# Layer 0 of a two-layer cross-attention kernel: transfers in another order, on other queues

## The chip, the cores and the metric

The kernel runs on one NeuronCore of a Trainium2 chip. Its time is the device time of one execution in microseconds (us). TensorE (PE in the profile; PEld is its weight loading) does the matmuls and the transposes, VectorE (DVE), ScalarE (ACT) and GpSimd (POOL) work element by element, and SyncE (SP) only issues DMAs. ScalarE issues DMAs as well, between its own instructions. Each of the two has a queue of its own, `q1` for SyncE and `q10` for ScalarE; 16 DMA engines serve both. Engines wait for one another through semaphores.

## The reference

Two layers run one after the other on a batch of 8 sequences, `x` (8, 112, 512), with a context `ctx` (8, 375, 512). All is float32. Layer 0 is a grouped-query cross-attention with 32 query heads and 8 key/value heads of 16 elements:

```python
q = x @ Wq + bq ; k = ctx @ Wk + bk ; v = ctx @ Wv + bv
scores = einsum('bkgld,bksd->bkgls', q, k) * 0.25 + mask
out = einsum('bkgls,bksd->bkgld', softmax(scores), v)
x = layernorm(out @ Wo + bo + x) * gamma + beta
```

Layer 1 is two cross-attentions of 16 heads with 128 elements, each on a layer norm of `x`, and a GELU MLP with 2048 hidden units, with residuals. It is about nine tenths of the time, and the change doesn't touch its arithmetic.

## The kernel before

**Tiling.** The batch is done in two halves (`hf` 0 and 1) of four sequences, one after the other, and each half runs layer 0, both attentions of layer 1 and the MLP. For float32 accuracy each operand is split into a high and a low part (`_hi`, `_lo`), and a product is three matmuls (lines 794 to 796). Weights come into two slots of `raw`; GpSimd splits them (lines 674 and 676) and frees the slot, which the next load awaits.

**Layer 0 before its loop.** TensorE works through a list of units, written out by hand (`pre_order`): `n` transposes of the context ("natural" layout), `k` keys of a sequence, `q` a quarter of the queries (one 128-column piece of Wq each), `vt` and `v` values. ScalarE takes the high part of each result and VectorE the low part. For the first half the list is `n0 k0 n1 k1 n2 vt0 k2 q0 vt1 v0 n3 q1 vt2 v1 k3 q2 vt3 v2 q3 v3`, for the second `k0 q0 k1 q1 vt0 q2 vt1 v0 k2 q3 vt2 v1 k3 vt3 v2 v3`. Keys and queries are then rearranged through DRAM: `store_keys0` (line 440, four DMAs) and `store_queries0` (line 455, two DMAs) write scratch tensors, and `load_keys0` (line 449) and `load_queries0` (line 474, four DMAs) read them back in the layout of the scores. A store waits for its unit; a load waits for its store to land. SyncE issues all of these, the loads of the weights (line 418) and the mask (line 498) in the order in which they are written, so one that waits holds those behind it. The first load of queries also waits for a memset of `qo` on GpSimd (line 661), which comes after the splits of Wq. A store of the natural layout (`nat_scratch`, 1536 KB) goes out on ScalarE's queue (line 1251). ScalarE frees `keys` buffers by waiting for the earlier stores to land.

**The layer-0 loop.** It has 128 steps `n`, 32 for each of four chunks `c`, eight for each sequence `b` of a chunk. In a step TensorE forms the scores of one head and transposes the probabilities of an earlier one, VectorE takes the maximum (line 1730), ScalarE the exp (line 1331), and each second step ScalarE and VectorE move two transposed heads into a buffer `pt0` (lines 1177 and 1566). There are two such buffers of four heads, used in turn: number 0 is `pt_hi`/`pt_lo`, where pieces 1 to 3 of the queries stood before (`q0_split`), number 1 lies in `rr`, where two of the natural stages stood. So ScalarE waits at step 1 until all stores of queries have landed, and at step 4 until the natural stores have, in the first half also the write of the extra values (`bx_scratch`, line 574). Each eight steps GpSimd scales a batch of outputs (line 685). The keys and queries of a later chunk are loaded once TensorE has read the same sequence of the chunk before, 24 steps ahead of their use.

**The second half's inputs.** In the first half the context and the tokens of the second are copied inside DRAM (`ctx_copy`, 3000 KB, line 585; `x_copy`, 896 KB, line 487), on SyncE's queue behind the loads of the second chunk; they are read back at the end of layer 1. There ScalarE splits the tokens (`split_x`), and at the end of the half stores `out` (line 1556) and then the last natural stage.

## Time and profile before

| | us |
|---|---|
| median of 3 runs | 2464.18 |
| lowest and highest | 2464.01, 2466.08 |
| the profiled execution | 2464.88 |
| its span, first to last instruction | 2463.0 |
| TensorE busy | 2320.6 |
| VectorE busy | 1401.3 |
| ScalarE busy | 999.3 |
| GpSimd busy | 765.6 |

Mean granted TensorE clock: 0.981 of full speed. The first half starts at 0 and its layer-0 loop at 69; the second starts at about 1254 and its loop at about 1290. A timeline line gives the start, the busy time, the engine, the line, what is written from what, and in brackets the idle time before it with what ended it. A line of SPq or ACTq is a DMA issue: the time is that of issuing, not of the transfer. A line of windows gives the busy time of each engine in a stretch, then the granted clock, the mean busy share of the 16 DMA engines and their GB/s.

### The profile page before, as it was taken

The numbers are of one execution on the slowest core, as the hardware profiler recorded it, in microseconds if no ns is written. First come the engines' busy times: TensorE is split into PE (matmuls) and PEld (weight loads), VectorE is DVE, ScalarE is ACT, GpSimd is POOL, SyncE is SP. The second block draws the span as 40 slices with busy tenths as digits, with TensorE's granted clock in tenths as the row PEclk, the third lists the DMA queues.
The fourth block names the chain that finished last, engine by engine and source line by source line (L and its number), as shares of the span: only waits on it lengthen the run. The fifth ranks groups of instructions, "written<-read, shape, count | busy, mean of one in ns | idle before, by whom it ended". The sixth has DMA issues, their size and how long they took to land. (4 is left out here: it accounts for less than half of the span.)

```text
span 2463.0 us, 36589 instructions
## 1 busy us (share of the span) xinstructions
PE 2320.6 (94%) x13464; PEld 2087.0 (85%) x13464; DVE 1401.3 (57%) x3146; ACT 999.3 (41%) x2195; POOL 765.6 (31%) x823
## 2 busy tenths in 40 slices
PE   6898899999999999998988979999999999999998
PEld 5666899998989999997876769998989999998976
DVE  4687645454565455456548965455546655454574
ACT  3685433243433333243238944243334333243420
POOL 2132322415141423313531331414141422415055
PEclk9899999999999999999999989999999999999999
DMA  8351323233323323234363213333332323233222
GB/s 279 96 156 39 92 85 108 87 91 116 99 86 96 95 82 111 82 96 146 125 198 96 77 40 95 97 101 97 103 95 82 96 90 107 86 87 121 79 76 79
DMA packets 134533, 250.46 MB, mean 102 GB/s; under 512 B 31151, under 2 KB 54831, under 8 KB 133335
## 3 DMA queue, kind: packets, MB, share of 16 engines
q1 hardware_dynamic: 90863, 125.37, 17.0%
q10 hardware_dynamic: 43496, 122.76, 16.2%
q8 instruction: 110, 1.80, 0.3%
q14 instruction: 64, 0.52, 0.1%
HBM read 223.19 MB, written 29.48 MB: 103 GB/s over the span
## 5 line engine op out<-in xcount | busy, mean ns | idle before, releaser
L674 POOL TENSOR_SCALAR wk_hi<-raw 128x512 fp32r<-128x512 f32 (+1 forms) x84 | 54.0, 643 | 905.5 <-DMA raw<-in_wk 747.5
L1411 ACT ACTIVATE probs<-scores,prm 112x376 f32<-112x376 f32 x256 | 147.1, 575 | 342.9 <-DVE prm L1805 342.8
L794 PE MATMUL pj_two<-ctx_hi,wk_hi 128*128 128x376 f32 x708 | 243.6, 344 | 7.7 <-DVE rr L1566 4.1
L1566 DVE TENSOR_TENSOR rr<-pj_two,rr 128x448 fp32r<-128x448 f32 (+2 forms) x223 | 147.0, 661 | 172.6 <-ACT rr L1177 172.2
L795 PE MATMUL pj_two<-ctx_lo,wk_hi 128*128 128x376 f32 x708 | 239.0, 338 | 0.0
L796 PE MATMUL pj_two<-ctx_hi,wk_lo 128*128 128x376 f32 x708 | 238.5, 337 | 0.0
L794 PE MATMUL pj_two<-pt_hi,nat 125*128 125x448 f32 x531 | 198.8, 374 | 10.6 <-issue 10.2
L676 POOL TENSOR_TENSOR wb_lo<-raw,wb_hi 128x512 fp32r<-128x512 f32 x152 | 197.9, 1302 | 12.7
L1568 DVE SCALAR_TENSOR_TENSOR k_lo<-pj_two,cur,k_hi 128x375 fp32r<-128x375 f32 x167 | 101.3, 607 | 173.1 <-ACT k_hi L1179 172.6
L796 PE MATMUL pj_two<-pt_hi,nat 125*128 125x448 f32 x531 | 195.4, 368 | 0.0
L795 PE MATMUL pj_two<-pt_lo,nat 125*128 125x448 f32 x531 | 195.2, 368 | 0.0
L1179 ACT ACTIVATE k_hi<-pj_two,cur 128x375 fp32r<-128x375 f32 x167 | 95.6, 573 | 228.4 <-PE pj_two L796 223.6
L799 PE MATMUL tp_two<-ident,probs 112*126 112x112 f32 (+1 forms) x1152 | 163.0, 266 | 25.8 <-ACT probs L1331 12.2
L799 PEld LDWEIGHTS tp_two<-ident,probs 112*126 112x126 f32 (+1 forms) x1152 | 146.2, 160 | 47.7 <-DVE probs L1813 15.7
L1177 ACT ACTIVATE rr<-pj_two 128x448 fp32r<-128x448 f32 (+2 forms) x223 | 127.4, 572 | 129.6 <-PE pj_two L796 110.9
L1566 DVE TENSOR_TENSOR pt_lo<-tp_two,pt_hi 126x336 fp32r<-126x336 f32 (+1 forms) x288 | 144.2, 537 | 24.7 <-ACT pt_hi L1177 24.7
L674 POOL TENSOR_SCALAR wb_hi<-raw 128x512 fp32r<-128x512 f32 x152 | 98.8, 650 | 188.9 <-DMA raw<-in_wv 76.8
L1805 DVE TENSOR_REDUCE prm<-scores 112x1 f32<-112x376 f32 x256 | 138.5, 541 | 21.7 <-PE scores L796 21.7
L1331 ACT ACTIVATE probs<-probs,prm 112x375 f32<-112x375 f32 x256 | 146.9, 602 | 2.6 <-DVE prm L1730 2.6
L794 PEld LDWEIGHTS pj_two<-ctx_hi,wk_hi 128*128 128x128 f32 x708 | 134.5, 190 | 9.9 <-issue 4.5
L676 POOL TENSOR_TENSOR wo<-raw,wo 128x512 fp32r<-128x512 f32 x104 | 139.0, 1337 | 8.7
L1177 ACT ACTIVATE pt_hi<-tp_two 126x336 fp32r<-126x336 f32 (+1 forms) x288 | 123.5, 478 | 42.5 <-PE tp_two L799 29.1
(278 smaller groups left out, 6611.1 us busy)
## 6 DMA issues: line engine op xcount, KB each, us to landing
nat<-nat_scratch ACTq DMA_DIRECT2D x256, 384.0 KB, 3.7
raw<-in_wq SPq DMA_DIRECT2D x72, 256.0 KB, 3.3
raw<-in_wo SPq DMA_DIRECT2D x72, 256.0 KB, 2.6
raw<-in_wk SPq DMA_DIRECT2D x64, 256.0 KB, 3.8
raw<-in_wv SPq DMA_DIRECT2D x64, 256.0 KB, 4.2
raw<-in_w SPq DMA_DIRECT2D x64, 256.0 KB, 2.9
nat_scratch<-rr ACTq DMA_DIRECT2D x7, 1536.0 KB, 8.8
k_hi<-keys_scratch SPq DMA_DIRECT2D x32, 188.0 KB, 2.8
```

The source lines that it names most:

```text
L674: nc.gpsimd.tensor_scalar(hi, src, 1.0, 0.0, ALU.mult, ALU.add).then_inc(split_hi, 1)
L676: nc.gpsimd.tensor_tensor(lo, src, hi.bitcast(F32), ALU.subtract).then_inc(signal, k)
L794: nc.tensor.matmul(dst, l_hi, r_hi, start=first, stop=False)
L795: nc.tensor.matmul(dst, l_hi, r_lo, start=False, stop=False)
L796: return nc.tensor.matmul(dst, l_lo, r_hi, start=False, stop=last)
L799: return nc.tensor.transpose(dst, src, ident[0:parts, 0:parts])
L1177: i = nc.scalar.activation(dst, src, ACT.Copy)
L1331: nc.scalar.activation(probs[0:L, n % 4, 0:S], probs[0:L, n % 4, 0:S], ACT.Exp, bias=neg_max[0:L, n % HPC:n % HPC + 1], scale=-1.0).then_i ...
L1411: nc.scalar.activation(probs[0:L, h, 0:SK], scores[n % SCR][0:L, 0:SK], ACT.Exp, bias=neg_max[0:L, h:h + 1], accum_out=row_sum[0:L, h:h + ...
L1566: i = nc.vector.tensor_tensor(dst, src, hi.bitcast(F32), ALU.subtract)
L1568: i = nc.vector.scalar_tensor_tensor(dst, src, bias, hi.bitcast(F32), ALU.add, ALU.subtract)
L1805: nc.vector.tensor_reduce(neg_max[0:L, h:h + 1], scores[n % SCR][0:L, 0:SK], AX_X, ALU.max, negate=True).then_inc(max_ready, 1)
```

## The change

It has six parts. In the first half SyncE issues the loads of Wq's pieces 1 to 3 each between the earlier stores and loads of keys, and the mask and the bias rows later; the stores of the queries come before the last load of keys. In the second half the load of queries comes before the store of keys 1, and each store of queries one place earlier. The two copies inside DRAM leave SyncE and are issued by ScalarE at step 24 of the first half's loop. The buffers `pt0` are used in the other order in the second half, and ScalarE's waits at steps 1 and 4 are exchanged there. The last natural stage is stored before `out`. All arithmetic is the same.

```diff
                     store_keys0(0, *pre_split("k", 0))
+                    load_q0(base + RAW_Q, 1)
+                    store_keys0(1, *pre_split("k", 1))
+                    load_q0(base + RAW_Q + 1, 2)
+                    load_keys0(0, 0)
+                    load_q0(base + RAW_Q + 2, 3)
+                    load_keys0(0, 1)
                     sp.dma_start(rows8_dram[0], bias_v).then_inc(rows8_in, 16)
                     sp.dma_start(rows8_dram[1], bv).then_inc(rows8_in, 16)
-                    store_keys0(1, *pre_split("k", 1))
-                    load_q0(base + RAW_Q, 1)
-                    load_keys0(0, 0)
-                    load_keys0(0, 1)
+                    store_keys0(2, *pre_split("k", 2))
+                    store_queries0(0, *pre_split("q", 0))
 
                     sp.wait_ge(pj_free, pre_freed("n", 2, SC - 1) + PJ)
                     load_mask()
-                    load_q0(base + RAW_Q + 1, 2)
-                    store_keys0(2, *pre_split("k", 2))
-                    store_queries0(0, *pre_split("q", 0))
-                    load_q0(base + RAW_Q + 2, 3)
                     load_queries0(0, 0)
...
                     store_queries0(1, *pre_split("q", 1))
+                    store_queries0(2, *pre_split("q", 2))
                     store_keys0(3, *pre_split("k", 3))
-                    store_queries0(2, *pre_split("q", 2))
+                    store_queries0(3, *pre_split("q", 3))
                     load_keys0(0, 3)
-                    store_queries0(3, *pre_split("q", 3))
                 else:
...
                     load_keys0(0, 0)
+                    load_queries0(0, 0)
+                    store_queries0(1, *pre_split("q", 1))
                     store_keys0(1, *pre_split("k", 1))
-                    load_queries0(0, 0)
                     load_mask()
-                    store_queries0(1, *pre_split("q", 1))
+                    store_queries0(2, *pre_split("q", 2))
                     load_keys0(0, 1)
-                    store_queries0(2, *pre_split("q", 2))
+                    store_queries0(3, *pre_split("q", 3))
                     store_keys0(2, *pre_split("k", 2))
-                    store_queries0(3, *pre_split("q", 3))
                     load_keys0(0, 2)
...
-                        if hf == 0:
-                            sp.dma_start(ctx_dram, ctx_t[:, HB:B, :]).then_inc(ctx_copied, 16)
-                            copy_x(1)
...
-                    p_hi, p_lo = (t[0:KC, :, s * L:(s + 1) * L] for t in pt0[u % 2])
+                    p_hi, p_lo = (t[0:KC, :, s * L:(s + 1) * L] for t in pt0[(u + hf) % 2])
...
-                    if n == 1:
+                    if n == (1, 4)[hf]:
 
                         for t in q0_out:
                             act.wait_ge(t, (hf + 1) * 32)
-                    if n == 4:
+                    if n == (4, 1)[hf]:
...
+                    if n == 24 and hf == 0:
+
+                        act.dma_start(ctx_dram, ctx_t[:, HB:B, :]).then_inc(ctx_copied, 16)
+                        act.dma_start(x_dram[:, T:2 * T], x_t[:, T:2 * T]).then_inc(x_copied, 16)
...
                             split_x(1)
+                            store_nat(1, m, mpj + mu["n", SC - 1] + 1)
...
-                if hf == 0:
-                    store_nat(1, HB - 1, at["mlp"] + (MLPG - 1) * MLP_U[0] + mu["n", SC - 1] + 1)
```

SyncE's queue in the first half, from the stores of keys 0 on. `raw<-in_wq` is a piece of Wq, `keys_scratch` a store of keys, `queries_scratch` one of queries (`rr` is piece 0), `k_hi` and `qo` are loads of keys and queries, `xacc<-in_mask` is the mask. Before:

```order
L440 DMA keys_scratch<-wk_hi 8x16x376 x4
L525 DMA bias_rows_scratch<-in_bias_v 16x256
L526 DMA bias_rows_scratch<-in_bv 16x256
L440 DMA keys_scratch<-wk_lo 8x16x376 x4
L418 DMA raw<-in_wq 128x4x128
L449 DMA k_hi<-keys_scratch 128x376 x2
L498 DMA xacc<-in_mask 112x4x375
L418 DMA raw<-in_wq 128x4x128
L440 DMA keys_scratch<-wk_hi 8x16x376 x4
L455 DMA queries_scratch<-rr 8x16x448 x2
L418 DMA raw<-in_wq 128x4x128
L474 DMA qo<-queries_scratch 32x4x448 x4
```

And with the change:

```order
L440 DMA keys_scratch<-wk_hi 8x16x376 x4
L418 DMA raw<-in_wq 128x4x128
L440 DMA keys_scratch<-wk_lo 8x16x376 x4
L418 DMA raw<-in_wq 128x4x128
L449 DMA k_hi<-keys_scratch 128x376
L418 DMA raw<-in_wq 128x4x128
L449 DMA k_hi<-keys_scratch 128x376
L531 DMA bias_rows_scratch<-in_bias_v 16x256
L532 DMA bias_rows_scratch<-in_bv 16x256
L440 DMA keys_scratch<-wk_hi 8x16x376 x4
L455 DMA queries_scratch<-rr 8x16x448 x2
L498 DMA xacc<-in_mask 112x4x375
```

The three pieces of Wq have moved up among the first two stores and loads of keys, and the mask stands behind the first store of queries.

SyncE's queue in the second half, from the load of keys 0 to the load of keys 2. Here `pt_hi` and `pt_lo` are the two parts of the query pieces 1 to 3. Before:

```order
L449 DMA k_hi<-keys_scratch 128x376
L440 DMA keys_scratch<-wk_lo 8x16x376 x4
L474 DMA qo<-queries_scratch 32x4x448 x4
L498 DMA xacc<-in_mask 112x4x375
L455 DMA queries_scratch<-pt_hi 8x16x448
L455 DMA queries_scratch<-pt_lo 8x16x448
L449 DMA k_hi<-keys_scratch 128x376
L455 DMA queries_scratch<-pt_hi 8x16x448
L455 DMA queries_scratch<-pt_lo 8x16x448
L440 DMA keys_scratch<-wk_hi 8x16x376 x4
L455 DMA queries_scratch<-pt_hi 8x16x448
L455 DMA queries_scratch<-pt_lo 8x16x448
```

And with the change:

```order
L449 DMA k_hi<-keys_scratch 128x376
L474 DMA qo<-queries_scratch 32x4x448 x4
L455 DMA queries_scratch<-pt_hi 8x16x448
L455 DMA queries_scratch<-pt_lo 8x16x448
L440 DMA keys_scratch<-wk_lo 8x16x376 x4
L498 DMA xacc<-in_mask 112x4x375
L455 DMA queries_scratch<-pt_hi 8x16x448
L455 DMA queries_scratch<-pt_lo 8x16x448
L449 DMA k_hi<-keys_scratch 128x376
L455 DMA queries_scratch<-pt_hi 8x16x448
L455 DMA queries_scratch<-pt_lo 8x16x448
L440 DMA keys_scratch<-wk_hi 8x16x376 x4
```

The last store of queries now precedes the four DMAs of keys 2, and the load of queries those of keys 1.

ScalarE where the halves meet, from the splits of the context and the tokens to the first keys of the second half. Before:

```order
L1220 ACTIVATE ctx_hi<-ctx_lo 128x4x375
L1225 ACTIVATE h_hi<-pt_hi 128x896
L1225 ACTIVATE h_hi<-pt_lo 128x896
L1556 DMA out<-xacc 112x4x512
L1251 DMA nat_scratch<-rr 128x3072
L1179 ACTIVATE wk_hi<-pj_two,prm 128x376
```

And with the change:

```order
L1217 ACTIVATE ctx_hi<-ctx_lo 128x4x375
L1222 ACTIVATE h_hi<-pt_hi 128x896
L1222 ACTIVATE h_hi<-pt_lo 128x896
L1248 DMA nat_scratch<-rr 128x3072
L1558 DMA out<-xacc 112x4x512
L1176 ACTIVATE wk_hi<-pj_two,prm 128x376
```

The natural store and the store of `out` have changed places; `out` alone waits for the last sums of the MLP.

## Rows read from the trace of the kernel before

**Rows 1.** The page: busy time, share of the span and instructions of each engine.

```profile
PE 2320.6 (94%) x13464; PEld 2087.0 (85%) x13464; DVE 1401.3 (57%) x3146; ACT 999.3 (41%) x2195; POOL 765.6 (31%) x823
```

**Rows 2.** Waits of TensorE: us in total, times, longest us.

```profile
PE tp_two L799 <- ACT probs L1331: 12.2, 2, 7.4
...
PE pj_two L794 <- POOL wb_lo L676: 6.7, 2, 3.7
```

**Rows 3.** Timeline of TensorE, layer 0 of both halves: start, busy us, what.

```profile
62.74 0.71 PE L794 MATMUL pj<-h_hi,wb_hi 128*128 128x448 f32 x1 [5.15 <-POOL wb_lo L676]
...
69.47 0.59 PE L930 MATMUL scores<-k_hi,qo 128*112 128x376 f32 x2 [1.27 <-DVE k_lo L1566]
...
1268.75 0.44 PE L794 MATMUL pj_two<-h_hi,wb_hi 128*128 128x448 f32 x1 [3.66 <-POOL wb_lo L676]
```

**Rows 4.** Timeline of GpSimd, first half, splits of Wq.

```profile
41.70 0.87 POOL L674 TENSOR_SCALAR wb_hi<-raw 128x512 fp32r<-128x512 f32 x1 [20.06 <-DMA raw<-in_wq]
...
60.63 0.62 POOL L674 TENSOR_SCALAR wb_hi<-raw 128x512 fp32r<-128x512 f32 x1 [8.76 <-DMA raw<-in_wq]
```

**Rows 5.** Timeline of SyncE's DMA issues, first half.

```profile
36.01 5.31 SPq L449 DMA_DIRECT2D k_hi<-keys_scratch  x2
...
46.84 1.57 SPq L455 DMA_DIRECT2D queries_scratch<-rr  x2
48.45 0.58 SPq L418 DMA_DIRECT2D raw<-in_wq  x1
59.90 1.76 SPq L474 DMA_DIRECT2D qo<-queries_scratch  x4
...
69.77 0.88 SPq L455 DMA_DIRECT2D queries_scratch<-pt_lo  x1
74.70 0.36 SPq L449 DMA_DIRECT2D k_hi<-keys_scratch  x1
```

**Rows 6.** Timeline of ScalarE, both halves.

```profile
80.79 0.73 ACT L1177 ACTIVATE pt_hi<-tp_two 125x672 fp32r<-125x672 f32 x1 [7.96 <-DMA queries_scratch<-pt_lo]
...
1255.24 0.51 ACTq L1251 DMA_DIRECT2D nat_scratch<-rr  x1
...
1298.49 0.73 ACT L1177 ACTIVATE pt_hi<-tp_two 125x672 fp32r<-125x672 f32 x1 [5.37 <-DMA queries_scratch<-pt_lo]
```

**Rows 7.** Timeline of GpSimd, first half's loop: one batch of outputs each.

```profile
129.52 0.40 POOL L685 TENSOR_TENSOR xacc<-xacc,prm 112x128 f32<-112x128 f32 x1 [3.63 <-DVE xacc L1739]
137.81 0.40 POOL L685 TENSOR_TENSOR xacc<-xacc,prm 112x128 f32<-112x128 f32 x1 [3.75 <-DVE xacc L1739]
148.57 0.41 POOL L685 TENSOR_TENSOR xacc<-xacc,prm 112x128 f32<-112x128 f32 x1 [10.36 <-DVE xacc L1739]
158.20 0.41 POOL L685 TENSOR_TENSOR xacc<-xacc,prm 112x128 f32<-112x128 f32 x1 [9.22 <-DVE xacc L1739]
```

**Rows 8.** DMA issues from 110 to 150: KB each, median us to landing.

```profile
ctx_copy<-in_ctx_t SPq DMA_DIRECT2D x1, 3000.0 KB, 15.0
```

**Rows 9.** Windows: us, PE, PEld, DVE, ACT, POOL busy, clock, DMA share, GB/s.

```profile
1250.00:1255.00 5.00, 5.00 (x25) 4.04 (x24) 3.12 (x8) 0.00 (x0) 3.25 (x4) 1.00 0.20 55
...
1260.00:1265.00 5.00, 5.00 (x28) 4.58 (x26) 1.29 (x2) 1.21 (x2) 0.00 (x0) 1.00 0.99 308
...
1270.00:1275.00 5.00, 5.00 (x21) 4.65 (x20) 0.68 (x1) 0.64 (x1) 3.87 (x2) 0.70 0.58 186
```

**Rows 10.** Timeline of GpSimd, second half: third piece of Wq, memset of the queries.

```profile
1266.64 0.62 POOL L674 TENSOR_SCALAR wb_hi<-raw 128x512 fp32r<-128x512 f32 x1 [6.98 <-DMA raw<-in_wq]
...
1270.93 3.09 POOL L661 MEMSET qo<- 128x3584 f32 x1 [0.15 <-POOL wb_lo L676]
```

**Rows 11.** Timeline of SyncE's DMA issues behind the copies and in the second half.

```profile
128.35 7.75 SPq L474 DMA_DIRECT2D qo<-queries_scratch  x4
...
1274.10 2.64 SPq L474 DMA_DIRECT2D qo<-queries_scratch  x4
...
1288.72 0.89 SPq L455 DMA_DIRECT2D queries_scratch<-pt_lo  x1
```

More of the change, by code:

```diff
@@ L1360, in _ @@
                         two = n // 2
-                        move(pt0[n // 4 % 2][0][0:KC, n % 4 - 1:n % 4 + 1, :], twos[two % 2][0:KC, :, 0:SC * L],
+                        move(pt0[(n // 4 + hf) % 2][0][0:KC, n % 4 - 1:n % 4 + 1, :], twos[two % 2][0:KC, :, 0:SC * L],
                              two_ready, two0 + two + 1, mid=two_mid)
@@ L1758, in _ @@
                         two = n // 2
-                        hi, lo = (p[0:KC, n % 4 - 1:n % 4 + 1, :] for p in pt0[n // 4 % 2])
+                        hi, lo = (p[0:KC, n % 4 - 1:n % 4 + 1, :] for p in pt0[(n // 4 + hf) % 2])
                         lo_of(lo, twos[two % 2][0:KC, :, 0:SC * L], hi, two_mid, two0 + two + 1, two_free)
```

## The prediction

> **What bounds the kernel now.** The page comes first [rows 1]: TensorE is busy 94% of the span, so time is to be had only where it stands idle or runs slowly. The waits of TensorE, largest in total first, then say for whom [rows 2]: 12.2 us in two waits for ScalarE's exps (longest 7.4), 6.7 us in two waits for GpSimd's splits of Wq (longest 3.7), and a third such wait on another buffer, below. All sit in the layer-0 stages at the start of either half. The timelines of the engines there give the causes.
>
> First half. TensorE waits 3.0 us at 41.1 (6.7 less the longest, 3.7) and 5.15 us at 57.6 for split columns of Wq [rows 2, 3]; GpSimd had waited 20.06 and 8.76 us for the raw columns to land [rows 4], because SyncE issues these loads behind stores of keys, the last one at 48.45 [rows 5]. The attention loop starts at 69.47 [rows 3] and stops at once: ScalarE waits 7.96 us at step 1 for the last queries store, which SyncE issues behind the load of keys 3 (74.70, [rows 5]), and goes on at 80.79 [rows 6]. In the loop GpSimd scales one batch each 8.3 us (129.52 to 137.81); the next two come 10.76 and 9.63 us apart [rows 7]. There the copies for the second half, 15.0 us to landing [rows 8], stand in SyncE's queue ahead of the keys and queries of the third chunk. The excess is 2.5 + 1.3 = 3.8 us.
>
> Second half. The last natural store leaves at 1255.24, right behind `out` [rows 6]; the share of the DMA engines is 0.20 before it and 0.99 after [rows 9]. GpSimd waits 6.98 us for the third piece of Wq [rows 10], TensorE 3.66 us for the split [rows 3], and its granted clock is 0.70 in the next 5 us against 1.00 in the 5 us that end as the wait begins [rows 9]. Then ScalarE waits 5.37 us at step 1 of the loop for the last queries store [rows 6], issued at 1288.72 [rows 11].
>
> **Part by part.** Positive is time saved.
>
> 1. First half, loads of Wq in front. Columns 1 are issued right behind the stores of keys 0. SyncE's queue is served about in order, and these stores had landed when the load that waits for them could go, at 36.01 [rows 5]. So columns 1 land near 37 instead of 41.7, are split some 2.2 us later [rows 4], and the wait of 3.0 goes. Columns 3 leave at about 36.4 instead of 48.45, and the wait of 5.15 goes. TensorE would reach the loop near 60. It can't use all of it: the loop needs the first queries from DRAM. Their store, issued at 46.84, had landed when SyncE issued the load, at 59.90 [rows 5], and the new order does not issue it earlier, since the landing of keys 1 stands ahead of it as before. But the mask (0.67 MB) no longer lies in front of it, and natural store 3 on ScalarE's queue comes 3 us earlier. I take 3.4 us: the load at 56.5.
>
> 2. First half, stores of queries in front of the load of keys 3. SyncE's issues end at 70.65 and go on at 74.70, when keys 3 has landed [rows 5]; the last queries store follows that. Now it goes ahead of it, and of the 4 us I take 2.6, since its bytes still queue. Items 1 and 2: 3.4 + 2.6 = **6.0 us**. Lower bound: 2.6 alone. Upper bound: both TensorE waits, 3.0 + 5.15, and a little clock, 9. Next in line are the extra values, which ScalarE awaits at step 4; their write follows the load of keys 3, now near 71 to 74 with landing near 77, and ScalarE gets there at about 78. There is no margin, so I stay at 6.0.
>
> 3. Copies on ScalarE's queue, at step 24 of the first loop, some 25 us after its start. SyncE's queue is rid of 3.9 MB, and the 3.8 us of [rows 7] go. The loads that now run beside the copies are those of the second chunk's last sequences. SyncE issues each as soon as its buffer is free, 24 steps ahead of its use, 25 us at 8.3 us for eight steps, and even the whole copy takes only 15.0 us to land [rows 8]. So they hide. The new cost is the issuing: the natural store took ScalarE 0.51 us to issue [rows 6], two such are 1.0; I take 0.9, all of it lost, as ScalarE is one of the engines that set the loop's pace. Net **2.9 us**, between 0 (loads still late) and 3.8 (issues hidden). Here the Trainium skill speaks against the change: DMA: Bandwidth & Descriptors, section Issuing engines are not separate DMA queues, says that transfers started by scalar and sync run on the same 16 engines and interleave, and that a second issuer saves only the time of issuing. By that rule the copies take the same bandwidth from the loads wherever they are issued. No copy on ScalarE's queue in the trace of before could show it; it is weighed as a rival.
>
> 4. Natural store in front of `out`. ScalarE issues it right after the token splits, near 1246, ahead of the stretch with a share of 0.20 [rows 9]. Nothing waits for its condition: its pieces were finished before. It takes 1.5 MB out of the stretch from 1255 to 1265, where Wq's pieces 2 and 3 are loaded. Against it, pieces 0 and 1 of Wq and Wv now load beside it, 2 to 3 us later, and about 1.3 us of wait could appear at piece 1. Of the 3.66 us and some 1.5 us of low clock (0.30 of 5 us) I take 3.5. The memset of the query rows, 1270.93 plus 3.09 [rows 10], ends when SyncE's load of queries leaves, 1274.10 [rows 11]; both move up by 3.3 us.
>
> 5. Second half, order of the stores and swapped buffers. At step 1 ScalarE now fills the buffer in `rr`, which needs only the natural stores, long landed; the queries' stores it needs at step 4, 3.3 us later. Before, from the load of queries to the landing of the last queries store: 3.9 MB from 1274.10 to 1298.4, 24.3 us, 160 GB/s. In the new order keys 1's stores come into that stretch and keys 2's leave it; the bytes are the same. From 1270.8 that gives 1295.1. The mask, with 2.8 MB up to its end at the same rate, lands at 1288.2 and lets the loop start then, 1.9 us sooner than VectorE's 1290.1; step 4 is reached at 1295. Before, it was reached at 1298.5 + 3.3 = 1301.8. Items 4 and 5: 1301.8 - 1295.1 = **6.7 us**. Lower bound: nothing gained before the loop, the last store landed at 1298.4 as before, 3.4. Upper bound: 5.37 + 3.66, 9. Next in line are keys 2 at step 16, landed at about 1299.5 and needed at 1302.
>
> Sum: 6.0 + 2.9 + 6.7 = **15.6 us**. The profiled execution took 2464.88 us, its span and 1.9 around it; that is 0.7 above the median of 2464.18. 2464.9 - 15.6 = **2449.3 us**. The stages behind are untouched and follow one another on TensorE, so what is gained at the start of a half arrives at the end.
>
> **Rivals.**
>
> Bytes decide, 2456.0. The stretches are bound by the flow through SyncE's queue, and another order of the same bytes moves the last landing little. For it: a share of 0.99 [rows 9] and 24.3 us for 3.9 MB. Against it: the hole in SyncE's queue from 70.65 to 74.70. Price: the lower bounds of both stages, 2.6 + 2.9 + 3.4 = 8.9.
>
> The copies still hurt, 2453.1. They slow the loads of the second chunk as they did those of the third, and the 3.8 us are not gained: 2464.9 - 15.6 + 3.8. Against it stand the 25 us of lead. This is what the skill's rule on issuing engines would give.
>
> New waits take the place, 2460. ScalarE waits at step 4 of the first loop for the extra values, TensorE at step 16 of the second for keys 2, each 5 to 6 us: left are 1 + 2.9 + 1. Against it: each producer also moves up.
>
> Slower, 2471.3. ScalarE's queue does not take the second copy until much of the first is through, and every us in which it holds ScalarE is lost to the loop. For it: on SyncE, four small loads behind the copies took 7.75 us to issue [rows 11]. Price: held for 20 us (15.0 to landing, and more beside other loads), and 2 us of low clock after it, with 0.9 for the issues, against 6.0 + 3.8 + 6.7: 2464.9 + 22.9 - 16.5. It decides from about 13 us of holding. Against it: SyncE issued the second copy without such a stop.
>
> **How the numbers follow.** Forecast 60%; bytes decide 20%; copies still hurt 8%; new waits 8%; slower 4%. The range leaves out the last two: its upper end, 2459, is 2464.9 less all lower bounds, 2.6 + 0 + 3.4; its lower end, 2443, less all upper bounds, 9 + 3.8 + 9. A measurement of this kernel can tell about 0.2%, 4.9 us, from no change, so faster means under 2459.3. The first three cases are faster, 88%; new waits is the same, 8%; slower 4%.
>
> **What the changed profile would show.** Item 1: no TensorE wait for a split of Wq in the first half, loop start at 61 to 66. Item 2: ScalarE's step 1 at 73 to 77. Item 3: batches 8.3 us apart throughout, one by under 1.5 us longer after the copies. Item 4: TensorE's wait for the third piece under 1.5 us, the share from 1250 to 1255 (less what the first half saves) near 0.9. Item 5: ScalarE at step 4 within 7 us of the loop's start. The prediction is wrong if the first queries store lands no earlier, if ScalarE takes over 2 us to issue the copies, or if its wait at step 4 of either half is over 3 us.

## The result

| | before | changed |
|---|---|---|
| median, 19 runs each | 2464.18 us | 2455.36 us |
| lowest, highest | 2457.64, 2472.16 | 2448.16, 2465.56 |
| profiled span | 2463.0 | 2453.3 |
| mean granted TensorE clock | 0.981 | 0.985 |

The ratio is 0.9964, with a 95% interval of 0.9955 to 0.9973: 8.9 us faster, between 6.7 and 11.1. The forecast was 15.6 us. Sign and range (2443 to 2459) were right, the size was not.

To see where the time went, five points of the two traces are compared. The first and the last batch that GpSimd scales mark a loop (as in [rows 7]), and the unit of keys 0 on ScalarE marks the start of the second half.

| us | before | changed | difference |
|---|---|---|---|
| first batch of loop 1 | 96.41 | 96.59 | +0.2 |
| loop 1, first to last batch | 124.24 | 120.42 | -3.8 |
| from there to keys 0 of the second half | 1035.48 | 1037.61 | +2.1 |
| from keys 0 to the first batch of loop 2 | 57.24 | 46.84 | -10.4 |
| loop 2 | 120.40 | 120.40 | 0 |
| from there to the end | 1029.23 | 1031.44 | +2.2 |
| span | 2463.0 | 2453.3 | -9.7 |

The third and the sixth row, mostly layer 1, are 84% of the span, somewhat less than the nine tenths given at the start.

Engine totals hardly move against [rows 1]; the work is the same. From the page of the changed kernel:

```profile
PE 2311.3 (94%) x13464; PEld 2078.5 (85%) x13464; DVE 1401.8 (57%) x3146; ACT 998.9 (41%) x2195; POOL 766.4 (31%) x823
```

**First half: nothing gained.** SyncE's issues in the changed kernel; they answer to [rows 5]:

```profile
22.84 11.67 SPq L440 DMA_DIRECT2D keys_scratch<-wk_lo  x4
34.55 0.77 SPq L418 DMA_DIRECT2D raw<-in_wq  x1
...
44.78 0.34 SPq L449 DMA_DIRECT2D k_hi<-keys_scratch  x1
...
49.98 2.98 SPq L455 DMA_DIRECT2D queries_scratch<-rr  x2
...
61.99 1.74 SPq L474 DMA_DIRECT2D qo<-queries_scratch  x4
...
74.02 0.87 SPq L455 DMA_DIRECT2D queries_scratch<-pt_lo  x1
78.68 0.36 SPq L449 DMA_DIRECT2D k_hi<-keys_scratch  x1
```

Piece 1 of Wq now stands in front of the stores of keys 1, and these four took 11.67 us to issue, against 9.31 before (10.6 to 14.0 in the six profiles with this order, 8.1 to 10.7 in the three with the old one). The load that waits for them goes at 44.78, and the queries of chunk 0 are stored at 49.98 instead of 46.84 and loaded at 61.99 instead of 59.90. TensorE, and then ScalarE at steps 1 and after, show what that means:

```profile
68.83 0.94 PE L927 MATMUL scores<-k_hi,qo 128*112 128x376 f32 x2 [9.07 <-DMA qo<-queries_scratch]
```

```profile
80.98 0.73 ACT L1174 ACTIVATE pt_hi<-tp_two 125x672 fp32r<-125x672 f32 x1 [8.36 <-DMA queries_scratch<-pt_lo]
```

Both waits of TensorE for splits of Wq are gone, as forecast. In their place stands one of 9.07 us for the queries themselves, and step 1 is as late as in [rows 6].

**Loop 1.** GpSimd's batches, at the place of [rows 7], and ScalarE's issues of the copies:

```profile
129.75 0.41 POOL L682 TENSOR_TENSOR xacc<-xacc,prm 112x128 f32<-112x128 f32 x1 [2.11 <-DVE xacc L1739]
138.03 0.40 POOL L682 TENSOR_TENSOR xacc<-xacc,prm 112x128 f32<-112x128 f32 x1 [3.72 <-DVE xacc L1739]
146.32 0.41 POOL L682 TENSOR_TENSOR xacc<-xacc,prm 112x128 f32<-112x128 f32 x1 [7.88 <-DVE xacc L1739]
```

```profile
105.23 0.59 ACTq L1364 DMA_DIRECT2D ctx_copy<-in_ctx_t  x1
105.86 0.63 ACTq L1365 DMA_DIRECT2D x_copy<-in_x_t  x1
```

Up to the last two, which are closer together in both kernels, all batches are 8.3 us apart. The whole 3.8 us are gained in this pair of profiles, and the 1.2 us of issuing cost nothing that can be seen. That is not so in every execution: in four later profiles the second copy took ScalarE 1.29 to 1.79 us to issue instead of 0.63, and one batch came 0.7 to 1.2 us late. One of them is of the changed kernel with another order only in its second half:

```profile
104.18 1.47 ACTq L1365 DMA_DIRECT2D x_copy<-in_x_t  x1
```

**Second half.** ScalarE stores natural early, at 1238.47, while SyncE is still issuing the loads of Wk (1233.59 to 1240.78). Then Wk lands later, GpSimd waits 5.45 us for it (1.41 before), and VectorE's low parts of Wk stand ahead of its last MLP sums, for which TensorE waits. GpSimd, then TensorE:

```profile
1246.04 0.41 POOL L698 TENSOR_SCALAR wk_hi<-raw 128x256 fp32r<-128x256 f32 x1 [5.45 <-DMA raw<-in_wk]
```

```profile
1247.87 0.48 PE L791 MATMUL pj_two<-wo,qo 128*112 128x512 f32 x1 [2.33 <-DVE xacc L1616]
```

The wait for the third piece of Wq [rows 3] is gone, as forecast, but the idle stretch of the DMA engines is only moved, and the low clock stands behind the new wait (0.66, against 0.70 in [rows 9]):

```profile
1248.00:1253.00 5.00, 5.00 (x17) 3.81 (x18) 3.03 (x4) 0.00 (x0) 3.72 (x3) 0.66 0.20 56
```

Behind that, on ScalarE: a new wait at the unit of keys 3, and step 1 without the 5.37 us of [rows 6]:

```profile
1280.13 0.57 ACT L1176 ACTIVATE wk_lo<-pj_two,prm 128x376 fp32r<-128x376 f32 x1 [3.86 <-DMA keys_scratch<-wk_lo]
...
1287.54 0.73 ACT L1174 ACTIVATE rr<-tp_two 125x672 fp32r<-125x672 f32 x1 [0.38 <-PE tp_two L796]
```

### The profile page after: what moved, and what is told of

The parts are those of the page before. It is cut to its first block and busy times, and to the rows that moved or that the text cites. A ratio compares the mean times of both kernels' runs of the same rounds, so it can differ in the third digit from the quotient of the medians.

```text
span 2453.3 us, 36589 instructions
## 1 busy us (share of the span) xinstructions
PE 2311.3 (94%) x13464; PEld 2078.5 (85%) x13464; DVE 1401.8 (57%) x3146; ACT 998.9 (41%) x2195; POOL 766.4 (31%) x823
## 5 line engine op out<-in xcount | busy, mean ns | idle before, releaser
L1730 DVE CUSTOM_DVE_ANT_0 probs<-scores,xacc 112x375 f32<-112x375 f32 x256 | 133.4, 540 | 12.9 <-PE scores L927 12.9
```

The lines of the kernel that those rows point to most:

```text
L1730: nc.vector.tensor_tensor_reduce(probs[0:L, n % 4, 0:S], scores[n % SCR][0:L, 0:S], mask_v[:, n // HPC % HB, :], -1.0, 3.0e38, ALU.add, AL ...
```

## The experiments

Two theories stood at the start: the order in SyncE's queue decides (then another order of the first half must pay), or the bytes do, whatever their order. Single profiles of kernels with the same start differ by up to 2.6 us at the first batch, and those with the same order at the change of halves by up to 5.5 us in the stretch of some 1035 us ahead of it, so totals and stretches of single profiles are read with that in mind, and means of several or the waits themselves are preferred. Of the experiments, those with stores by channel were run four times each and the one with the natural store put back ten times, the others once.

### One store earlier still

The first queries are stored ahead of keys 2, of the load of keys 1 and of the bias rows.

```diff
+                    store_queries0(0, *pre_split("q", 0))
+                    store_keys0(2, *pre_split("k", 2))
                     load_keys0(0, 1)
                     sp.dma_start(rows8_dram[0], bias_v).then_inc(rows8_in, 16)
                     sp.dma_start(rows8_dram[1], bv).then_inc(rows8_in, 16)
-                    store_keys0(2, *pre_split("k", 2))
-                    store_queries0(0, *pre_split("q", 0))
```

> The changed kernel, but in the first half the store of queries 0 comes ahead of the store of keys 2, and both come ahead of the load of keys 1 (which waits for the landing of keys 1, 44.78 in the changed kernel). Theory: that landing held the store of queries 0 (49.98) and so the first load of queries (61.99) and the loop. Then the store goes out at 39 to 41, the load of queries at 50 to 56, the loop starts at 60 to 63 (TensorE is ready at about 60), ScalarE passes step 1 at 73 to 76 instead of 80.98, and the first batch of outputs is scaled at 89 to 92 instead of 96.59. Rival, bytes decide: the queue is bound by its flow; the load goes at 58 or later and the first batch is within 2 us of 96.6.

Measured: one run of 2450.13 us; the first batch at 94.06. The store goes at 39.33 instead of 49.98 and the load at 52.35 instead of 61.99, 9.6 us earlier, yet TensorE still waits for it, until 65.76:

```profile
65.76 0.94 PE L927 MATMUL scores<-k_hi,qo 128*112 128x376 f32 x2 [8.37 <-DMA qo<-queries_scratch]
```

SyncE's last queries store is issued at 68.53 and ScalarE goes on at 78.46. Issued at 52.35, the four loads took 7.2 to 11.2 us to land. Of 9.6 us in the order 2.0 to 2.5 arrive at the first batch (94.06, against a mean of 96.03 over four profiles with the changed order, or 96.59), hardly more than the spread. The first theory is right on the issues and wrong on all that follows them: mostly the second. Something other than the order limits the flow.

### The copies at another time

```diff
-                    if n == 24 and hf == 0:
+                    if n == 44 and hf == 0:
```

> The changed kernel, but ScalarE issues the two copies at step 44 of the first loop, about 126 us, the time at which SyncE issued them before. It asks whether the queue or the time took the 3.8 us out of the loop. The loop from its first to its last batch took 124.2 us before and 120.4 in the changed kernel. If the queue decides (the loads of the third chunk no longer stand behind the copies but share the engines with them), 120.4 to 121.5. If only the time decides (same engines, same bytes beside the loads with the short lead), 123 to 125.

Measured: one run of 2460.97 us; loop 1 takes 120.53 us, against 120.42 with the copies at step 24. They are issued at 124.67 and 125.30, where SyncE issued them at 126.33 and 126.96 in the kernel before, beside the loop's loads, and hurt nothing in the loop. So it was SyncE's queue, in which four small loads stood behind them (7.75 us to issue, [rows 11]), and not the traffic. Beside the copies, but on another queue, the slowest four of these loads took 4.78 us to issue. The Trainium skill (DMA: Bandwidth & Descriptors, section Issuing engines are not separate DMA queues) says that a second issuer saves only the time of issuing, which is usually small beside the transfer. Read as in the rival, that nothing is gained in the loop, it is not borne out here: the loop is 3.7 us shorter in this profile. SyncE's time of issuing did fall, from 7.75 to 4.78 us, so a part of what was saved is of the kind that the rule names, but it was not small.

### The natural store alone, the second half's order alone

Two kernels, each the kernel before with one part of the change. First part 4, the store behind the last token split (its old place is taken out):

```diff
                             split_x(1)
+                            store_nat(1, m, mpj + mu["n", SC - 1] + 1)
```

> The kernel before with one part of the change: the last natural store in front of out. Theory: it delays the loads of Wk, Wq and Wv for the second half, GpSimd's split, VectorE's second part of Wk and with it the last sums of the MLP behind it on VectorE. From the last batch of the first loop to ScalarE's first keys of the second half it takes 1035.5 us before and 1037.6 in the changed kernel; here 1038 to 1041, and TensorE waits 2 to 3 us for VectorE's sums near 1250. From those keys to the loop's first batch it takes 57.2 before and 46.8 changed; here the wait for the third piece of Wq goes, 51 to 54, with the wait at step 1 still there. Rival: the store costs nothing there and the 4 us are run-to-run variation of layer 1: 1033 to 1036.

Measured: one run of 2465.82 us beside 2468.11 of the kernel before. From loop 1's last batch to keys 0 it took 1039.71 us (before 1035.48), from there to loop 2 54.61 (before 57.24). As expected, TensorE no longer waits for the third piece of Wq. The cost seen in the changed kernel is there, and step 1's wait stays:

```profile
1251.44 0.49 PE L794 MATMUL pj_two<-wo,qo 128*112 128x512 f32 x1 [2.35 <-DVE xacc L1615]
```

```profile
1297.57 0.73 ACT L1177 ACTIVATE pt_hi<-tp_two 125x672 fp32r<-125x672 f32 x1 [7.83 <-DMA queries_scratch<-pt_lo]
```

Then part 5, the order of the second half's stores with the exchanged pairs:

```diff
                     load_keys0(0, 0)
+                    load_queries0(0, 0)
+                    store_queries0(1, *pre_split("q", 1))
                     store_keys0(1, *pre_split("k", 1))
-                    load_queries0(0, 0)
...
-                    if n == 1:
+                    if n == (1, 4)[hf]:
```

> The kernel before with one part of the change: the order of the stores and loads in the second half and the swapped buffers with their waits. From ScalarE's first keys of the second half to the loop's first batch it takes 57.2 us before and 46.8 changed. Theory: the wait at step 1 (5.4) goes, the wait for the third piece of Wq (3.7, and low clock) stays: 50 to 53. Rival: without the natural store out of the way the stores of queries land as late as before and the wait moves to step 4: 54 to 56.

Measured: one run of 2460.26 us beside the same 2468.11. The stretch from keys 0 to loop 2 takes 52.45 us instead of 57.24, 4.8 less, although TensorE's wait for the third piece of Wq (3.90 us) is still there. ScalarE no longer waits at step 1 and waits 3.79 us at keys 3, as in the changed kernel.

The 2.3 us of TensorE go with the moment at which the early store leaves. Over all runs with it, in six profiles it left while SyncE was still issuing the loads of Wk; GpSimd then waited 5.45 to 5.77 us for Wk, and TensorE 2.33 to 2.36 us for `xacc` in the five of them with VectorE in its old order. In two it left right behind the last of these loads (1239.79 against 1239.67 in the kernel with the first store of queries moved up); there the wait for `xacc` is 0 and 0.17 us. So much only shows that the two go together: no run moved the store for this alone.

### The natural store put back, and VectorE's low parts put behind its sums

The first is the changed kernel without part 4:

```diff
-                            store_nat(1, m, mpj + mu["n", SC - 1] + 1)
...
+                if hf == 0:
+                    store_nat(1, HB - 1, at["mlp"] + (MLPG - 1) * MLP_U[0] + mu["n", SC - 1] + 1)
```

> The changed kernel with one part undone: the last natural store of the second half is issued behind the output again. Theory A (the prediction's term: the early store is worth 3.5 us at TensorE's wait for the third piece of Wq): 3 to 4 us slower than the changed kernel, and that wait is back. Theory B (the store in front costs about as much ahead of the second half as it gives behind it): within 1.5 us of the changed kernel; the distance from loop 1's last batch to the first keys unit 2 to 3 us shorter than in the changed kernel, the stretch from there to loop 2 longer by as much.

Measured: 2454.74 us over ten runs, ratio to before 0.9974 (0.9962 to 0.9985), against 0.9964 with the early store. By the medians part 4 is worth -0.6 us, by the ratios +2.5, and the two intervals overlap; the 3.5 us of the forecast are not there. Its profile has 1032.20 us up to keys 0 and 51.08 behind; the first theory's sign, the wait for the third piece, comes back with only 0.45 us, and TensorE waits 2.20 us for the second piece instead. The sum of the two stretches is 1084.45, 1087.21, 1091.67 and 1087.54 us in the four profiles with both parts 4 and 5 and stores by head (the changed kernel, the first two experiments and the one with the pairs exchanged in both halves), 1089.30 and 1083.28 in the two with part 5 alone: means of 1087.7 and 1086.3.

The second leaves the store early and takes away the cause of TensorE's wait:

```diff
                         split_x(1)
-                        wk0_rest(1)
...
+                    if hf == 0 and m == MLPG - 1:
+                        wk0_rest(1)
```

> The changed kernel, with VectorE's low parts of Wk for the second half moved behind its four output sums of the last MLP group instead of ahead of them. Theory A (storing natural early cost 2 to 4 us because Wk landed later and VectorE's sums stood behind its low parts): the wait of TensorE for VectorE's xacc at 1247 to 1251 (2.33 us) is gone, and from the last batch of loop 1 to ScalarE's first keys unit there are 1034.5 to 1037 us instead of 1037.6 to 1040.4; the time falls by about 2 us. Theory B (the bytes decide: TensorE waits as long for Wk's own low parts, or for the next piece of Wq): the wait only moves to the keys unit or the queries units and that distance stays in 1037.6 to 1040.4.

Measured: one run of 2461.24 us. The wait for xacc is gone and keys 0 come after 1035.29 us, but the stretch behind grew from 46.84 to 56.27. Both theories missed this. VectorE's low parts free the slots of `raw`, so the next loads, Wq's first piece and Wv, leave SyncE at 1250.13 and 1250.77 instead of 1241.95 and 1247.06, and ScalarE has its first queries only at 1263.33 instead of 1257.03:

```profile
1250.13 0.37 SPq L418 DMA_DIRECT2D raw<-in_wq  x1
1250.77 8.17 SPq L418 DMA_DIRECT2D raw<-in_wv  x2
```

```profile
1263.33 0.64 ACT L1176 ACTIVATE rr<-pj,prm 128x448 fp32r<-128x448 f32 x1 [9.52 <-PE pj L793]
```

### The exchanged pairs in the first half too

```diff
-                    if n == (1, 4)[hf]:
+                    if n == 4:
                         for t in q0_out:
...
-                    if n == (4, 1)[hf]:
+                    if n == 1:
-                        for i in range(2 if hf else 3):
+                        for i in range(2):
...
+                    if n == 4 and hf == 0:
+                        act.wait_ge(nat_out[2], 16)
+                        act.wait_ge(bx_out, 48)
```

> The changed kernel, with the order of the two pairs of probability tiles exchanged in the first half too: steps 0 to 3 write the pair that lies in rr, and only step 4 waits for the queries' stores. Theory A (in the first half what holds step 1 is the landing of the last queries store, 8.36 us of ScalarE's wait at 80.98, and the step could go at about 77): step 1 begins at 76 to 78.5, step 4 does not wait over 1 us, the first batch of loop 1 is at 91.5 to 94 instead of 95.2 to 96.6, the time falls by 2 to 4 us. Theory B (keys 3, whose load stands behind the same stores, or step 4's own wait come as late): the first batch stays in 94.5 to 97 and a wait shows at step 4 or at TensorE for k_hi.

Measured: one run of 2453.21 us; the first batch at 92.20. Step 1 goes at 72.05 without waiting, and the extra values are next in line, as the prediction had named them; on ScalarE:

```profile
72.05 0.73 ACT L1174 ACTIVATE rr<-tp_two 125x672 fp32r<-125x672 f32 x1 [0.38 <-PE tp_two L796]
...
81.25 0.61 ACT L1328 ACTIVATE probs<-probs,prm 112x375 f32<-112x375 f32 x1 [6.21 <-DMA bx_scratch<-k_lo]
```

Here 8.9 us at step 1 turn into 3.8 at the first batch. Loop 1 takes 1.2 us longer, since the second copy took ScalarE 1.79 us to issue; that is not the exchange's doing, as it also happens without it.

### The stores on all DMA engines

What limits the flow shows in a stretch in which hardly anything but stores of keys and queries runs. From 70 to 80 us (windows; columns as in [rows 9]), the kernel before and then the changed one:

```profile
70.00:80.00 10.00, 4.48 (x19) 3.82 (x18) 3.16 (x12) 2.18 (x4) 2.39 (x7) 0.75 0.54 171
```

```profile
70.00:80.00 10.00, 4.69 (x18) 4.20 (x18) 2.78 (x12) 2.21 (x4) 4.29 (x12) 0.67 0.53 192
```

A share of 0.53 to 0.54 with transfers waiting: as if half of the 16 engines stood idle. It is the same ahead of step 1 in the second half of the kernel before, where the stores of keys 2 and the last queries are written:

```profile
1284.00:1296.00 12.00, 8.71 (x41) 7.42 (x39) 4.89 (x15) 5.44 (x9) 0.00 (x0) 0.75 0.57 198
```

The scratch side of each store has 8 as its outermost count (heads), then 16 channels. The Trainium skill (DMA: Bandwidth & Descriptors, section Why a DMA increments its semaphore by 16 and not by 1) says that a DMA uses the largest number of engines up to 16 that divides the outermost counts of both sides. By that rule these stores have 8 engines; the trace agrees, with 0.53 to 0.57. To test it, the columns of Wq and Wk and their biases are laid out channel by channel, so that 16 can be outermost. Values and bytes are the same.

```diff
-  sp.dma_start(k_dram[hf, b, :, r, e, :, :], k0_split[b % 2][r].bitcast(F32))
+  sp.dma_start(k_dram[hf, b, :, r, e, :, :].rearrange("g d n -> d g n"), k0_split[b % 2][r].bitcast(F32))
...
-  sp.dma_start(q_dram[hf, c, :, e, :, :], q0_split[c][e].bitcast(F32))
+  sp.dma_start(q_dram[hf, c, :, e, :, :].rearrange("j d t -> d j t"), q0_split[c][e].bitcast(F32))
...
+    def by_channel(a):
+        s = a.shape[:-1]
+        return a.reshape(*s, -1, 8, HD0).swapaxes(-1, -2).reshape(*s, -1)
```

> The changed kernel, but the columns of Wq, Wk and their biases of the first attention are laid out channel by channel (16 channels, 8 heads in each) instead of head by head, so that the eight stores of a batch's keys and a chunk's queries can be issued with 16 as the outermost count instead of 8. Bytes, descriptors, loads and arithmetic stay the same. In the changed kernel the DMA share between 70 and 80 us, when only such stores run, was 0.54 at 188 to 197 GB/s. Theory A (a store whose outermost count is 8 is spread over 8 of the 16 DMA engines, and this is what kept the first half from gaining by an earlier store): the share in that stretch goes above 0.8 and the flow above 280 GB/s; ScalarE's step 1 begins before 77 instead of at 80.98; the first batch of loop 1 is at 89 to 93 instead of 95.2 to 96.6; the median falls by 4 to 9 us below the changed kernel's. Theory B (the stores are limited by memory or by the number of descriptors, not by how many engines serve them): the flow stays within 10% of 190 GB/s, step 1 stays within 1.5 us of 81, and the time within 2 us of the changed kernel's.

Measured: 2442.80 us, 12.6 below the changed kernel; ratio to before 0.9916 (0.9900 to 0.9931), against 0.9964 (0.9955 to 0.9973). The first batch comes at 81.04, 15.6 us earlier, which is more than even the first theory said, because the stores of keys 0 and 1 go faster too (SyncE loads keys 1 at 37.57 instead of 44.78) and between 70 and 76 nothing is left to write. From 57 to 63 nearly all that lands are stores of keys 3 and of queries, so this is the stretch to compare with 70 to 80 above; then step 1 on ScalarE:

```profile
57.00:63.00 6.00, 3.77 (x19) 2.98 (x18) 4.24 (x14) 3.18 (x6) 3.61 (x10) 0.87 1.06 379
```

```profile
65.94 0.73 ACT L1174 ACTIVATE pt_hi<-tp_two 125x672 fp32r<-125x672 f32 x1 [3.74 <-DMA queries_scratch<-pt_lo]
```

Share and flow are twice those of the stores by head, so the second theory, a limit of memory or of the number of descriptors, falls.

### The same stores in the kernel before

> The kernel before the change, in its own order of transfers, with its stores of keys and queries issued by channel (16 as the outermost count) as in e5_stores_by_channel. Against e5_stores_by_channel (first batch of loop 1 at 81.04, 2442.80 us) it is the whole change again, now with the stores out of the way. Theory A (the first half's order is worth the predicted 6 us once the stores do not limit it): the first batch is 4 to 7 us later than 81.04, loop 1 takes 124 instead of 121.2, and the time is 10 to 15 us above 2442.8. Theory B (in the first half the order is worth nothing even then): the first batch is within 1.5 us of 81.0, and the time 2 to 7 us above 2442.8 from the copies and the second half alone. Either way it should be 10 us or more under the kernel before, since only the stores' form differs.

Measured: 2444.04 us, ratio to before 0.9919 (0.9893 to 0.9946). That is 1.2 us above the changed order with the same stores, which is less than the runs of either differ among themselves, and less than the 2 to 7 us of the second theory. The first batch comes at 81.24 against 81.04, as that theory said, so the first half's order is worth nothing even now: with stores on 16 engines the kernel before does not wait for splits of Wq at all in its first half. From keys 0 (1237.08) to loop 2's first batch it takes 48.44 us, and 50.18 in the changed order; ScalarE no longer waits at step 1 of the second half, though order and buffers are the old ones there. What the changed order still gives in the profiles is the copies' part (loop 1 in 123.88 us, against 121.18); in the totals even that is not shown. The late batches are still there:

```profile
122.65 0.40 POOL L685 TENSOR_TENSOR xacc<-xacc,prm 112x128 f32<-112x128 f32 x1 [3.73 <-DVE xacc L1739]
133.13 0.40 POOL L685 TENSOR_TENSOR xacc<-xacc,prm 112x128 f32<-112x128 f32 x1 [10.08 <-DVE xacc L1739]
142.68 0.41 POOL L685 TENSOR_TENSOR xacc<-xacc,prm 112x128 f32<-112x128 f32 x1 [9.14 <-DVE xacc L1739]
```

### Combinations

All have the stores by channel and the changed order; the edits are those shown above.

> e5_stores_by_channel with steps 0 to 3 of the first half writing the pair in rr too, as in e7_other_pair_both_halves. There the step 1 wait went (72.05), and 6.21 us of wait for bx_scratch came at step 4. Theory A (the 3.74 us that ScalarE waits at step 1 in e5 for the last queries store can be had): first batch at 77.5 to 79.5 instead of 81.04, time 1.5 to 3.5 us below 2442.8. Theory B (the store of bx_scratch, which step 4 waits for, or the queries stores themselves take the place of that wait): first batch at 80.3 to 82, time within 1.5 us of 2442.8.

Measured: 2440.69 us, ratio 0.9908 (0.9888 to 0.9928). From the first exps (69.71) to the first batch (85.62) are 15.9 us, and 21.0 and 19.0 in the two profiles without the exchange (the second is of the next kernel). The profiled execution started its loop late, since GpSimd waited 11.04 us for a piece of Wv that it awaits 1.13 us in the kernel of the same start:

```profile
32.16 0.40 POOL L671 TENSOR_SCALAR wk_hi<-raw 128x256 fp32r<-128x256 f32 x1 [11.04 <-DMA raw<-in_wv]
```

> e5_stores_by_channel with the last natural store behind the output again, as in e8_natural_store_behind. Theory A (the early store only moves a cost, as e8 showed with 0.6 us between it and the changed kernel): within 1.5 us of 2442.8. Theory B (with stores on 16 engines the second half has room behind, and the cost of the early store ahead of it, 1039.3 us from loop 1's last batch to the first keys unit against 1032.2 in e8, is no longer given back): 3 to 6 us faster than 2442.8, that distance at 1032 to 1036.

Measured: 2439.06 us, ratio 0.9901 (0.9881 to 0.9921): 3.7 us faster by the medians, which is in the range of theory B, but the intervals overlap. The stretch up to keys 0 was 1037.36 us, as long as in the changed kernel and not 1032 to 1036, so the place that theory B named does not carry it. That it is not worse is all that can be said.

> The last kernel: stores by channel, the other pair in both halves, the copies on ScalarE's queue, the changed order of both halves, and the last natural store behind the output, so e11_by_channel_natural_behind (2439.06 us) with the exchange of e10_by_channel_other_pair. Theory A (the gains add: e10's profile waits at neither step 1 nor step 4, and from its first exponentials to the first batch there are 15.91 us, against 18.98 in e11): that distance is 15.5 to 16.5, the first batch at 76.5 to 78.5 if the loads of the weights land as in e11, and the median is 1.5 to 3.5 us below 2439.06, so 2435.5 to 2437.5. Theory B (what the exchange gives in the first half is lost in a wait at step 4 or in the spread of the layer behind it): within 1.5 us of 2439.06.

Measured: 2437.61 us, beside 2465.55 of the kernel before; ratio 0.9876 (0.9860 to 0.9893). It is 1.5 us under the one above, within theory B, and the two intervals overlap. In the profile 18.96 us pass from the first exps (61.24) to the first batch (80.20), as many as without the exchange, among them a wait of 2.46 us for the extra values. So with stores by channel the exchange in the first half is not shown to give anything. It is the fastest kernel of the study, by 26 to 35 us against before.

## Why the prediction was right in sign and too large

**Items 1 and 2, the failed step.** It is "I take 3.4 us: the load at 56.5" and the 2.6 behind it. The load went at 61.99, and step 1 at 80.98. Over all profiles with stores by head, the first batch is at 96.41, 94.57 and 97.14 in the three with the old order of the first half (mean 96.04), at 96.59, 95.17, 97.45 and 94.91 in the four with the new and nothing else changed in that half (mean 96.03). The 6.0 us are 0. The prediction's own condition for being wrong, that the first queries store lands no earlier, came true. Behind the step lies a reading: the waits for Wq were real, but the queue behind them was limited by its flow. The trace of before shows it, a share of 0.54 from 70 to 80 us, while stores were waiting; I had read only the hole in SyncE's issues there, from 70.65 to 74.70, and taken it for lost time. The new order even stores the first queries later, at 48.8 to 51.7 in the five profiles that have it unchanged, against 45.3 to 46.8 with the old one. The rival "bytes decide" named the cause in general and priced this item at 2.6.

**Item 3, right.** Forecast 2.9. The first pair of profiles has 3.8, but over all with stores by head loop 1 takes 124.24, 123.91 and 122.52 us with the copies on SyncE (mean 123.56), and 120.41 to 121.65 in the six with them on ScalarE (mean 120.80): 2.8 us. The charge for issuing, 0.9 us, was on the path in some executions and not in others. The rival that the copies still hurt falls, by the kernel with the copies at step 44. One sign of being wrong, over 2 us for issuing both copies, did come true in three profiles (0.59 and 1.47 to 1.79 us) and cost about 1 us.

**Item 4, mis-sized.** Its mechanism was right: the wait for the third piece of Wq is absent in all eight profiles with the early store. Its price was not. A wait at piece 1, "about 1.3 us", was named, but it was 3.85, 3.80 and 3.65 us in three profiles with stores by head, and 0 in the changed kernel's own, in which the gain looks whole:

```profile
1258.95 0.44 PE L791 MATMUL pj_two<-h_hi,wb_hi 128*128 128x448 f32 x1 [3.85 <-POOL wb_lo L673]
```

The path ahead of it, through Wk, VectorE's order and TensorE (2.3 us), was not foreseen at all. It goes back to a time: "near 1246" was the forecast for the store, ahead of the idle stretch of the DMA engines, and it left at 1242.02 with part 4 alone and at 1238.47 in the changed kernel (which is 3.6 us ahead there), in both 2.3 us before SyncE had issued the last load of Wk. Net about 0 instead of 3.5, by the ten runs with the store put back. VectorE's order can't simply be turned, as its low parts free the slots for the next loads.

**Item 5.** Step 1 no longer waits, and step 4 (1290.92) came 6.2 us after the loop's first exps (1284.75), as said. Behind keys 0 it is worth 4.8 us alone, in one pair of profiles, of 6.7 forecast for items 4 and 5 together. The wait at keys 3, 2.6 to 5.1 us, was not foreseen: the stores of keys 1 now go later, and that unit writes their buffer. The flow of 160 GB/s was taken from a count of 3.9 MB; the trace has 4.72 MB and 194 GB/s in that stretch, at a share of 0.57 where the last stores are written (1284 to 1296).

**The sum.** By the means over profiles, 0 for the first half, 2.8 for the copies, and 1092.7 - 1087.7 = 5.0 for items 4 and 5 (the first figure from the kernel before alone) give 7.8, measured 8.9 (6.7 to 11.1). The time lies next to that of the rival "bytes decide", 2456.0, but that is in part chance, as its parts were 2.6, 2.9 and 3.4. The rival of new waits was right that some would come, and had other places: the load of the queries in the first half, Wk, the second piece of Wq and keys 3 in the second. The slower rival had little for it: ScalarE was held by the second copy for 1.8 us at most, not for 13 or 20.

**Why there was something to gain.** The kernel before with faster stores is 1.2 us from the changed one with faster stores, and 18.6 us below itself. In the profile of the kernel before with faster stores ScalarE waits 3.43 us at step 1 of the first half and not at all in the second. So the gain of item 5 was part of a cost made by stores on half of the engines. Only the copies stand apart from it, with 2.8 us by the profiles; the totals of the two kernels with faster stores are too close, 1.2 us, to show it.

## What to carry to other kernels

Before transfers are put in another order, read the DMA share in a stretch in which the queue is full: near 0.5 with work waiting can be the mark of stores or loads that use half of the engines. Then test their form first; here it was worth 19 us, and the order and the queues 9. A wait that ends on a transfer moves with the queue's flow, not with the issue: of an issue moved up by 9.6 us, 2.0 to 2.5 arrived. A figure from one pair of profiles can hide a cost that comes in some executions only, as the issuing of the copies and the waits for Wk and the second piece of Wq do here. A large copy with much slack belongs on a queue on which nothing waits behind it.

## What the runs showed of the hardware

- Stores of 128 rows whose outermost count is 8 ran at a share of 0.53 to 0.54 and 171 to 192 GB/s; with 16 outermost the same bytes ran at 1.06 and 379 GB/s.
- Issuing depends on what stands in the queue: four stores of keys, right behind four others and a load of Wq, took SyncE 11.67 us to issue, and 9.31 with two small rows in place of the load; four took 3.54 at 46.40, and with 16 as the outermost count the crowded four took 8.71 us in the changed order and 3.94 in the old one.
- Copies of 3.9 MB on ScalarE's queue beside the loop's loads on SyncE's made no batch wait for these loads, at step 24 or 44. The second copy took 0.63 us to issue in six profiles and 1.29 to 1.79 in four.
- The landing of the first loads varies from run to run of the same code: 1.13 and 11.04 us of wait for the same piece of Wv, which moves everything behind it. What decides it stays open.
